# Stationary weights in the up projection of a routed expert stage, and a down projection that follows two slots later

## The reference, cut to what matters

```
x = layernorm(h)                                  # [tokens, 256], 16 * 255 tokens
gates = softmax(x @ w_red @ normalised(wg).T)     # 8 experts
idx, score = argmax(gates), max(gates)
a = gelu(x @ W1[idx] + b1[idx])                   # 256 -> 512, exact gelu
out = h + (a @ W2[idx] + b2[idx]) * score         # 512 -> 256
```

## Time and profile before

| | us |
|---|---|
| median of 3 runs | 721.15 |
| the profiled execution | 719.72 |
| its span | 718.0 |
| expert stage, first transpose of rows to last finish | 540.5 to 707.9 |
| PE busy in the span | 614.3 (86%) |
| DVE busy | 481.7 (67%) |
| ACT busy | 239.5 (33%) |
| POOL busy | 209.7 (29%) |

### The profile page before, as it was taken

One profiled execution on the slowest core, in us unless ns is written; L12 is line 12 of the kernel. 1 busy time (PEld: TensorE's weight loads), 2 busy tenths in 40 slices (PEclk: granted clock), 3 DMA queues, 4 the chain that ended last, 5 costly groups with the idle time before them and its releaser, 6 DMA issues. The chain is left out here.

```text
span 718.0 us, 12918 instructions
## 1 busy us (share of the span) xinstructions
PE 614.3 (86%) x3301; PEld 397.0 (55%) x3302; DVE 481.7 (67%) x1258; ACT 239.5 (33%) x475; POOL 209.7 (29%) x293
## 2 busy tenths in 40 slices
PE   3989999999999999999619988899327999999993
PEld 3757776666677776666314444444113565665652
DVE  2568888888888888888658778784582444444441
ACT  2124444434434444434410222222202333333430
POOL 7322222222222222122111112121042455554532
PEclk8999999999999999999965779796556999999998
DMA  9101110111111100110012223211001212222210
GB/s 253 38 30 59 59 42 16 58 58 58 58 58 58 58 30 29 58 59 29 30 39 89 68 68 91 86 51 37 23 1 44 59 61 63 61 62 62 64 49 0
DMA packets 30309, 39.85 MB, mean 56 GB/s; under 512 B 5090, under 2 KB 21731, under 8 KB 30288
## 3 DMA queue, kind: packets, MB, share of 16 engines
q1 hardware_dynamic: 21712, 26.04, 12.0%
q0 software_dynamic: 3744, 9.34, 4.5%
q10 hardware_dynamic: 4832, 4.21, 1.9%
HBM read 30.92 MB, written 9.59 MB: 56 GB/s over the span
## 5 line engine op out<-in xcount | busy, mean ns | idle before, releaser
L465 PE MATMUL banks<-proj,xnT_h 128*128 128x512 f16 x384 | 114.4, 379 | 13.8 <-DVE early L1055 13.8
L1492 POOL TENSOR_TENSOR sm<-sm,minus_half 128x1 f32<-128x1 f32 x64 | 40.9, 639 | 124.7 <-DVE sm L1026 83.4
L465 PE MATMUL banks<-proj,xnT_l 128*128 128x512 f16 x192 | 72.8, 379 | 0.0
L465 PEld LDWEIGHTS banks<-proj,xnT_h 128*128 128x128 f16 x384 | 36.3, 98 | 55.9 <-DVE early L1055 17.6
L1391 DVE TENSOR_TENSOR vo<-banks,vo 128x256 f16<-128x256 f32 x39 | 16.6, 425 | 70.9 <-ACT vo L871 70.9
L1572 POOL DMA_INDIRECT out<-proj,vo x39 | 39.6, 1016 | 79.7 <-DVE vo L1408 79.7
L440 PE MATMUL banks<-early 128*128 128x256 f32 x256 | 62.0, 385 | 0.7 <-ACT early L728 0.7
L442 PE MATMUL banks<-early 128*128 128x256 f32 x256 | 60.5, 379 | 0.0
L1496 POOL TENSOR_TENSOR w1l<-stage,w1h 128x512 f32 (+1 forms) x16 | 18.5, 1156 | 140.6 <-ACT w1h L772 140.6
L671 PE MATMUL banks<-w2h,vo 128*128 x312 | 57.5, 273 | 1.2 <-DVE proj L1406 1.2
L651 PE MATMUL banks<-w1h,vo 128*128 x156 | 55.0, 394 | 3.2 <-ACT vo L877 2.1
(11 more groups left out here) (258 smaller groups left out, 1370.4 us busy)
## 6 DMA issues: line engine op xcount, KB each, us to landing
early<-in_x SPq DMA_DIRECT2D x16, 512.0 KB, 4.3
stage<-in_W SPq DMA_DIRECT2D x32, 256.0 KB, 2.8
early<-lam_by_chunk SPq DMA_DIRECT2D x32, 132.0 KB
token_rows<-rows ACTq DMA_DIRECT2D x16, 129.0 KB, 2.3
token_rows<-rows ACTq DMA_DIRECT2D x16, 112.9 KB, 1.9
early<-in_tok_W SPq DMA_DIRECT2D x2, 512.0 KB, 8.4
early<-lam_by_head SPq DMA_DIRECT2D x16, 64.0 KB
vo<-token_rows,vo POOLq DMA_INDIRECT x39, 2.9
```

The source lines that it names most:

```text
L465: last = mm(dst, a, c, start=(i == 0), stop=(i == n - 1))
L1492: ptt(sm[:, dst:dst + 1], sm[:, src:src + 1], minus_half[:], ALU.pow).then_inc(s["rstd_ready"], 1)
```

## The change

- The up projection has the weights stationary and 128 columns of tokens moving. For each of four blocks of 128 features it issues six matmuls into bank 4 or 5. The result comes out as features by tokens, which is what down needs, so `transpose_gelu` is gone.
- The bias is now one number per partition. Four small matmuls ahead of the stage spread `b1` over slots into `b1_slot` (each slot's expert is compared with the expert's number, `expert_row`), and ACT adds it inside the gelu, which becomes four activations of 128 columns.
- ACT takes the high part of gelu from `gel` in SBUF, and DVE the low part. `xh` and `xl` have two buffers each.
- On PE the order in the step of slot i is: transpose rows of i+1, up(i), down(i-2). On DVE the split of gelu stands ahead of the split of rows. The numbers of the last two experts are carried in registers from round to round.
- POOL makes one small constant more; one DMA of `b1` replaces two.

```diff
-            def up(i, e):
+            def up(i, w, e):
 
                 pe.wait_ge(s["xdl_done"], i + 1)
-                if not (isinstance(i, int) and i == 0):
-                    pe.wait_ge(s["gelu_done"], i)
-                for c in range(DC):
-                    for x_, w in ((xh, w1h), (xh, w1l), (xl, w1h)):
-                        mm(bank(0), x_[:, c, :], w[:, bass.ds(e * DC + c, 1), :].rearrange("p a b -> p (a b)"),
-                           start=(c == 0 and w is w1h and x_ is xh), stop=False)
-                mm(bank(0), pick_expert[:, bass.ds(e, 1), :].rearrange("p a b -> p (a b)"), bias_hl[:, 0:FF],
-                   start=False, stop=True).then_inc(s["m1_ready"], 1)
-
-            def transpose_gelu(i, w):
-                pe.wait_ge(s["gelu_done"], i + 1)
                 if not (isinstance(i, int) and i < 2):
-                    pe.wait_ge(s["g_done"], i - 1)
+                    pe.wait_ge(s["gelu_done"], i - 1)
                 for f in range(FC):
-                    last = tr(bank(4 + w)[:, f * P:f * P + P], gel[:, f * P:f * P + P], ident[:])
-                last.then_inc(s["gt_ready"], 1)
+                    for c in range(DC):
+                        for w_, x_ in ((w1h, xh), (w1h, xl), (w1l, xh)):
+                            last = mm(bank(4 + w)[:, f * P:f * P + P],
+                                      w_[:, bass.ds(e * DC + c, 1), f * P:f * P + P].rearrange("p a b -> p (a b)"),
+                                      x_[:, w, c, :], start=(c == 0 and w_ is w1h and x_ is xh),
+                                      stop=(c == DC - 1 and w_ is w1l))
+                last.then_inc(s["m1_ready"], 1)
...
                 i0 = RING * g
                 experts = {0: expert_of(i0)}
+                if not first:
+                    for n in (-2, -1):
+                        experts[n] = pe.snap(carried_expert[n], min_val=0, max_val=E - 1)
                 for w in range(count):
-                    up(i0 + w, experts[w])
-
+                    if not (last and w == count - 1):
+                        transpose_rows(i0 + w + 1)
+                    up(i0 + w, w % 2, experts[w])
+                    if not (first and w < 2):
+                        down(i0 + w - 2, w % 2, experts[w - 2])
                     if w + 1 < count:
                         experts[w + 1] = expert_of(i0 + w + 1)
-                    if w < 2 and not first:
-                        experts[w - 2] = expert_of(i0 + w - 2)
-                    if not (last and w == count - 1):
-                        transpose_rows(i0 + w + 1)
-                    if not (first and w == 0):
-                        transpose_gelu(i0 + w - 1, (w - 1) % 2)
-                    if not (first and w < 2):
-                        down(i0 + w - 2, w % 2, experts[w - 2])
+                if not last:
+                    for n in (-2, -1):
+                        pe.reg_mov(carried_expert[n], experts[count + n])
...
             def gelu(i, w):
                 act.wait_ge(s["m1_ready"], i + 1)
                 if not (isinstance(i, int) and i == 0):
-                    act.wait_ge(s["gt_ready"], i)
-                af(gel, bank(0), ACT.Gelu).then_inc(s["gelu_done"], 1)
+                    act.wait_ge(s["g_done"], i)
+                for f in range(FC):
+                    last = af(gel[:, f * P:f * P + P], bank(4 + w)[:, f * P:f * P + P], ACT.Gelu,
+                              bias=b1_slot[:, f, bass.ds(i, 1)])
+                last.then_inc(s["gelu_done"], 1)
...
                 for w in range(count):
                     i = RING * g + w
+                    if not (first and w == 0):
+                        split_gelu(i - 1, (w - 1) % 2)
                     if not (last and w == count - 1):
-                        split_rows(i + 1)
+                        split_rows(i + 1, (w + 1) % 2)
                     if not (last and w >= count - 2):
                         norm_rows(i + 2, (w + 2) % RING, g if w + 2 < RING else g + 1)
-                    if not (first and w == 0):
-                        split_gelu(i - 1, (w - 1) % 2)
                     if not (first and w < 2):
                         finish(i - 2, (w - 2) % RING, g - 1 if w < 2 else g)
```

More of the change, by code:

```diff
@@ L232, in build @@
         xnD = over(D)
[L233 to L234 removed]
+        xh = over(D).bitcast(F16).rearrange("p (w c t) -> p w c t", w=2, c=DC)
+        xl = over(D).bitcast(F16).rearrange("p (w c t) -> p w c t", w=2, c=DC)
         gel = over(FF)
@@ L631, in _ @@
             last.then_inc(s["found_ready"], 1)
+            pe.wait_ge(s["expert_row_ready"], 1)
+            for f in range(FC):
+                last = mm(banks[:, 7, f * SLOTS:f * SLOTS + SLOTS], b1_rows[:, f * P:f * P + P], expert_row[:], start=True, stop=True)
+            last.then_inc(s["b1_ready"], 1)
             def transpose_rows(i):
@@ L866, in _, with split_rows, gelu, slots @@
             act.preload_act_table_set("gelu_and_others")
-            def split_rows(i):
+            act.wait_ge(s["b1_ready"], 1)
+            af(b1_slot[:].rearrange("p f i -> p (f i)"), banks[:, 7, 0:FC * SLOTS], ACT.Copy).then_inc(s["b1_done"], 1)
+            def split_rows(i, w):
                 act.wait_ge(s["xdt_ready"], i + 1)
-                if not (isinstance(i, int) and i == 0):
-                    act.wait_ge(s["m1_ready"], i)
-                af(xh.rearrange("p c t -> p (c t)"), bank(2, D), ACT.Copy).then_inc(s["xdh_done"], 1)
-            def gelu(i):
+                if not (isinstance(i, int) and i < 2):
+                    act.wait_ge(s["m1_ready"], i - 1)
+                af(xh[:, w].rearrange("p c t -> p (c t)"), bank(2, D), ACT.Copy).then_inc(s["xdh_done"], 1)
+            def gelu(i, w):
                 act.wait_ge(s["m1_ready"], i + 1)
                 if not (isinstance(i, int) and i == 0):
-                    act.wait_ge(s["gt_ready"], i)
-                af(gel, bank(0), ACT.Gelu).then_inc(s["gelu_done"], 1)
+                    act.wait_ge(s["g_done"], i)
+                for f in range(FC):
+                    last = af(gel[:, f * P:f * P + P], bank(4 + w)[:, f * P:f * P + P], ACT.Gelu,
+                              bias=b1_slot[:, f, bass.ds(i, 1)])
+                last.then_inc(s["gelu_done"], 1)
             def split_gelu(i, w):
-                act.wait_ge(s["gt_ready"], i + 1)
+                act.wait_ge(s["gelu_done"], i + 1)
                 if not (isinstance(i, int) and i < 2):
                     act.wait_ge(s["m2_ready"], i - 1)
-                af(gh[:, w].rearrange("p f t -> p (f t)"), bank(4 + w), ACT.Copy).then_inc(s["gh_done"], 1)
-            def slots(g, count=RING, first=False, last=False):
+                af(gh[:, w].rearrange("p f t -> p (f t)"), gel, ACT.Copy).then_inc(s["gh_done"], 1)
+            def slots(g, count=RING, last=False):
                 for w in range(count):
@@ L888, in slots @@
                     if not (last and w == count - 1):
-                        split_rows(i + 1)
-                    gelu(i)
-                    if not (first and w == 0):
-                        split_gelu(i - 1, (w - 1) % 2)
-            split_rows(0)
-            slots(0, first=True)
+                        split_rows(i + 1, (w + 1) % 2)
+                    gelu(i, w % 2)
+                    split_gelu(i, w % 2)
+            split_rows(0, 0)
+            act.wait_ge(s["b1_done"], 1)
+            slots(0)
             with act.Fori(1, ROUNDS) as g:
@@ L1528, in _ @@
             made.step(g.tensor_copy(place[:], ii[:, 0:P]))
+            made.settle()
+            made.step(g.iota(ii[0:E, 0:1], pattern=[[0, 1]], base=0, channel_multiplier=1))
+            made.settle()
+            made.step(g.tensor_copy(expert_no[:], ii[0:E, 0:1]))
             assert NTOK == 2 * P - 1
```

38 lines of the change are left out of this document (21 added, 17 removed).

## The result

| | before | changed |
|---|---|---|
| runs beside each other, median (lowest to highest), us | 720.95 (716.2 to 727.15), 4 runs | 743.2 (734.67 to 752.18), 4 runs |
| profiled execution, us | 719.72 | 742.26 |
| its span, us | 718.0 | 740.5 |
| its mean granted clock | 0.905 | 0.889 |

The ratio is 1.029, with an interval of 1.016 to 1.042: slower by 22 us in these runs. The forecast was 728.5, the range up to 741. A second set of runs of the same two kernels gave 732.41 (4 runs) against 721.82 (13 runs), a ratio of 1.016 (1.003 to 1.029). So the change costs about half of what the first runs showed.

The account below looks back on a forecast made before the run. PE bounds the expert stage before, its sequencer after. Prologue +0.1, start -1.6, steady part +9.3 and tail -0.5 give +7.3 us; with the runs' median of 721.15 the forecast is 728.5 us, range 716 to 741.

Parts of the forecast that it names:

- the prologue: Work ahead of the expert stage: one DVE compare on the path to the gathers, +0.1 us.
- The steady part: Expert stage from the fourth up to the last, 35 steps: 151.2 us against 141.9 before, +9.3.
- the start: First slots of the expert stage, up to the fourth up: -1.6 us (between -0.5 and -2.3).
- The sequencer becomes the bound: Expert slot: PE's register instructions need 4.27 us, above 4.04 before and PE's own 3.8; slot grows by 0.23 us.
- The tail: Expert stage from the last up's start to the last bias matmul: 8.3 us against 8.8 before, -0.5.
- PE's own time: PE's work in an expert slot: 1.89 + 24p, 3.19 to 4.51 us, taken as 3.8, below the sequencer's.
- p: Time of one 128x128 load with 128 columns in up: between 0.054 and 0.109 us, taken as 0.08.
- ACT: Gelu as four pieces of 0.28 us, 1.1 in all; ACT has 2.1 us in a slot of 4.27, covered.
- The cover: Expert slot: DVE's chain behind up takes 3.8 us, PE needs the result 5.5 us behind; covered by 1.7.
- Rivals: Matmuls at 0.109: 735.5, chance 0.08; clock falls: 740 to 750, chance 0.10; sequencer not binding: 712, chance 0.14.
- rival 2: Expert stage: granted clock falls to 0.9 to 0.8, +11 to +21 us, thus 740 to 750; chance 0.10.
- the group by +-0.01 us: Range term: uncertainty of one register group in the expert stage, over 12 x 35 groups, gives 4 us.

Follow-up runs that it names:

- the wide bias: Changed kernel with the down bias matmul over 128 rows (112 of them zeros) instead of 16; 729.64 us, ratio 1.011.
- Fixed addresses: Changed kernel with half, then all, of up's weight blocks read from expert 0 at fixed addresses; 714.56 and 715.35 us, ratio 0.987 each.
- the quarter columns: Kernel before with up's 512 columns issued as four times 128, 24 matmuls in place of six; 765.18 us against 726.87.
- the last version above: Kernel before with both bias matmuls over 128 rows, expert numbers carried in registers, and POOL's gather ahead of the scatter; 712.64 us, ratio 0.982.

## Why the prediction was wrong

**Right: the mechanism and the price of the stage.** I put the stage at +7.2 (the sum without the prologue); the two profiles of the changed kernel show +8.6 and +9.4, that with the wide bias +9.1. The steady part was put too low and the start too high, and the two misses cancel in part, which is luck. By its steps:

- *The sequencer becomes the bound.* Forecast 4.27 us a slot from eight and four groups at 0.25. Measured 4.35 on the average within the rounds. Fixed addresses (3.25) and the quarter columns (4.72) show the cause from both sides, and the wide bias shows that PE's work is off the path. The 0.08 above the forecast, in 25 steps, are 1.9 of the 2.6 us that the steady term missed; groups stand up to 0.28 apart, not 0.25. Another 0.9 lie in the five steps of the unrolled slots (4.26, 4.22, 4.52, 4.08 and 4.12, forecast 4.07).
- *The steady part*: 721.17 - 567.34 = 153.8 against a forecast of 151.2 and 141.9 before. +11.9, not +9.3. A round's start was put at 4.82; it is 4.73 to 4.76, and once 4.98.
- *The start*: from the first transpose to the fourth up 12.8 against 15.9. I had -1.6 (between -0.5 and -2.3), it is -3.1. This start spends 5.1 us at half clock (0.80 granted over 12.8 us), where before it spent 10.2 (0.68 over 15.9).
- *The tail*: 8.5 against 8.8; I had -0.5.
- *PE's own time.* I took p = 0.08; it is 0.057, for 24 matmuls 0.55 us less a slot than I took. It had no effect, as I had said, since the sequencer decides up to 0.099.
- *ACT.* I estimated 0.28 us for a gelu piece of 128 columns, 1.1 for the four. One record lasts 0.37, but they overlap: the four of a slot take 1.14, so the estimate was right. One slot, and all 156 records (busy us, then mean ns of one):

```profile
600.50 1.14 ACT L885 ACTIVATE vo<-banks,b_slot 128x128 f32<-128x128 f32 x4 [1.72 <-PE banks L661]
L885 ACT ACTIVATE vo<-banks,b_slot 128x128 f32<-128x128 f32 x156 | 44.6, 368 | 62.2 <-PE banks L661 61.6 <-DVE vo L1408 0.5
```

  ACT still has 11.2 busy us of 24, and within the loop PE waits neither for it nor for DVE. The cover held.
- *Rivals.* The clock of the stage stayed at 1.00, a matmul of 128 columns took 0.057 and not 0.109, and the sequencer binds: none of the three came true. But what rival 2 feared for the stage, a lower clock, happened ahead of it. What sets the grant no run shows: the stage kept 1.00 with PE busy for 21.95 of 24 us, and before it had 0.55 in its first 12 us and 1.00 later; that full work brought it back was my estimate.

**Wrong: the time outside the stage, taken as fixed.** The step that failed is the one that makes a median out of the sum: "The median of the runs is 721.15, 1.4 above the profiled execution", and a range made of "the group by +-0.01 us" and "the start 1". The rest of the program entered as a constant, with three runs behind it. It is none: the part from scan to router took 134.2 and 137.5 us in two executions of one kernel, 145.5 and 130.5 in two of the other, with the same instructions and the granted clock as the difference that shows (0.73, 0.71, 0.65 and 0.76). Of the 22 us measured first, about 9 are the stage. At equal time at half clock the kernels differ by 10.6: the start of the changed stage has about 4 us less at half clock (5.1 to 6.7 in three profiles, before 9.8 and 10.2), so at equal totals 4 us more lie elsewhere, by the slope an estimated 1.6. The other 12 us or so go with the low clocks of the first four runs, a mean of 0.887 against the 0.905 of the profiled execution before, at about 6 us for each 0.01; no clock is on record for the runs of the kernel before beside them. That these low clocks are no work of the change rests on its other four runs (0.896 to 0.913) and on the agreement of 732.5 and 733.0, not on a known cause of them. The view that could have told me was there: 0.78 granted between 460 and 480 us at 18.25 of 20 busy us. I used it only as a danger to the stage, and never asked how far it moves from run to run.

**What the forecast should have been**: 721.2 + 9.1, or 730, with a range some 10 us wider to both sides for the clock.

## What to carry to other kernels

Where addresses come from a register, count the distinct addresses as well as the matmuls: here each group of three matmuls cost the sequencer 0.25 us, whether they stream for 0.65 us or for 0.17, so smaller tiles with computed addresses can lose although PE has less to do. Before trusting a sum, ask how far the part that you don't touch moves by itself; where the clock varies, compare runs at equal time at half clock or stage by stage. And read the loads between the matmuls: an operand with few rows cost more here than one padded with zeros.

## What the runs showed of the hardware that I had not expected

- A 16-row weight load was not done ahead: about 0.1 us exposed before and behind each such matmul. Padding to 128 rows took a slot from 4.04 to 3.59 us.
- A load of six or eight values into PE's registers took a median of 1.00 to 1.01 us (0.59 to 2.19), one of a single value 0.30.
- Cut in four, a gelu of 512 columns took 1.14 us (four of 128, each with a bias per partition and 0.37 long by itself); in one piece, without a bias, it took 0.60.
- A 128-column fp16 matmul with its load took 0.057 us in a stream, where the fp32 one took 0.109.
- The clock granted in a stretch with the same instructions went from 0.59 to 0.76 between executions, and took its length from 155.1 to 130.5 us:

```profile
378.20:533.30 155.10, 140.62 (x416) 69.26 (x416) 98.72 (x328) 29.54 (x104) 25.14 (x32) 0.59 0.20 61
```

  This row is from the last version above, in a run at a mean clock of 0.864.
